# Search and mask rows made inside the top-32 attention, and GpSimd inverting the softmax sums of three attentions

## The reference, cut to what matters

```
x += softmax attention of layernorm(x) on ctx, with biases      l0a
x += mixture of 8 experts, one per token                        l0f
x += ctx aligned to layernorm(x) by dynamic time warping        dtw
x += gated feed-forward layer                                   l1f
x += softmax attention of layernorm(x) on ctx, rotary           l2a
x += mixture of 8 experts, two per token                        l2f
x += attention on ctx that keeps the 32 largest scores per row  l3a
x += attention of layernorm(x) on itself, in two groups         l3f
```

```
q, k, v = x @ W_qkv
sim = mean over the heads of cosine(q[token, head], g[head]), g given
sim = (sim - min) / (max - min)          # over all tokens but 5 registers per batch
pos = sim > 0.9
a token attends to the tokens of its own group and to the 5 registers;
a register's result is the mean of its results on both groups
```

## Time and profile before

| what | us |
|---|---|
| median of 3 runs | 2517.51 |
| lowest and highest run | 2512.94, 2529.06 |
| the profiled execution, its own time | 2528.44 |
| its span, first to last instruction | 2526.6 |

### The profile page before, as it was taken

How to read it: one execution, slowest core, us unless ns; L and a number is a source line. 1 busy time by engine, 2 the same in 40 slices (tenths; PEclk the granted TensorE clock), 3 DMA queues, 4 the chain that set the end, 5 groups by cost and what they waited for, 6 DMA issues and landing times. The chain is left out here.

```text
span 2526.6 us, 40368 instructions
## 1 busy us (share of the span) xinstructions
PE 1999.9 (79%) x13256; PEld 1620.2 (64%) x13256; DVE 1621.2 (64%) x5281; ACT 1161.8 (46%) x3231; POOL 1006.2 (40%) x939
## 2 busy tenths in 40 slices
PE   8996898699948967876999936777777777773887
PEld 5664798599827855555999925555655655562554
DVE  6765111588973246744111179999999999982884
ACT  3552232455321014432333336677777777672443
POOL 3310454300006033303555436666666666652540
PEclk9996999655879989987999956677877877676899
DMA  3111575520304012324364230000000000002232
GB/s 94 64 56 61 211 240 181 142 31 1 143 14 169 0 63 76 101 76 144 127 217 156 85 117 22 9 18 9 24 20 9 18 18 1 18 17 79 74 115 67
DMA packets 102803, 194.94 MB, mean 77 GB/s; under 512 B 20110, under 2 KB 71718, under 8 KB 94630
## 3 DMA queue, kind: packets, MB, share of 16 engines
q1 hardware_dynamic: 78792, 106.90, 13.2%
q0 software_dynamic: 23808, 85.50, 9.8%
HBM read 211.44 MB, written 50.10 MB: 104 GB/s over the span
## 5 line engine op out<-in xcount | busy, mean ns | idle before, releaser
L740 DVE MATCH_REPLACE8 l3a_left<-l3a_top,l3a_left 128x256 f32<-128x256 f32 x768 | 323.3, 448 | 0.0
L733 DVE MAX8 l3a_top<-l3a_left 128x8 f32<-128x256 f32 x768 | 300.1, 451 | 0.0
L466 POOL TENSOR_TENSOR l3a_prob<-l3a_expd,l3a_rest 128x512 f32<-128x512 f32 x128 | 162.9, 1273 | 219.9 <-ACT l3a_rest L548 219.3
L317 PE MATMUL l3a_psT<-all_ident,l3a_prob 128*128 128x128 f32 x512 | 112.5, 360 | 136.6 <-POOL l3a_prob L466 136.0
L335 PEld LDWEIGHTS l3a_psO<-l3a_probT,l3a_vp 128*128 128x128 f32 x1024 | 168.7, 247 | 69.8 <-ACT l3a_probT L564 40.2
L335 PE MATMUL l3a_psO<-l3a_probT,l3a_vp 128*128 128x128 f32 x1024 | 192.2, 346 | 26.0 <-ACT l3a_probT L564 26.0
L453 POOL TENSOR_TENSOR l3a_kept<-l3a_raw_sc,l3a_mone 128x512 f32<-128x512 f32 x128 | 163.4, 1276 | 67.9 <-ACT l3a_raw_sc L532 67.9
L1742 ACT ACTIVATE l2f_hT<-l2f_psH,l2f_wt 128x128 f32<-128x128 f32 x312 | 89.2, 369 | 213.2 <-PE l2f_psH L1673 186.3
L317 PEld LDWEIGHTS l3a_psT<-all_ident,l3a_prob 128*128 128x128 f32 x512 | 77.8, 183 | 155.7 <-POOL l3a_prob L466 155.7
L459 POOL TENSOR_TENSOR l3a_sc_sb<-l3a_kept,l3a_mlow 128x512 f32<-128x512 f32 x128 | 162.9, 1272 | 10.0
L2104 PE MATMUL dtw_psS<-dtw_r,all_shift 128*128 128x1 f32 x596 | 152.9, 357 | 9.8 <-DVE dtw_r L2284 9.4
(11 more groups left out here) (544 smaller groups left out, 4885.1 us busy)
## 6 DMA issues: line engine op xcount, KB each, us to landing
o_at<-l0a_oraw SPq DMA_DIRECT2D x16, 256.0 KB, 2.0
l0a_osum<-o_at SPq DMA_DIRECT2D x32, 128.0 KB
kv_at<-dtw_vd SPq DMA_DIRECT2D x8, 512.0 KB, 2.8
k_at<-dtw_kx SPq DMA_DIRECT2D x8, 512.0 KB, 4.0
l1f_kx<-k_at SPq DMA_DIRECT2D x8, 512.0 KB, 4.5
kv_at<-l1f_k SPq DMA_DIRECT2D x8, 512.0 KB, 3.1
l2a_k<-kv_at SPq DMA_DIRECT2D x8, 512.0 KB, 5.7
l2a_vd<-kv_at SPq DMA_DIRECT2D x8, 512.0 KB, 6.6
```

The costliest lines, as they stand in the source:

```text
L317: mm = nc.tensor.transpose(psT[u % 2][:, kc, e, :], prob[:, u % 4, e, kc * P:kc * P + P], ident[:])
L466: nc.gpsimd.tensor_tensor(prob[:, u % 4, :, :], expd[:, u % 2, :, :], rest[:, u % 2, :, :], ALU.subtract).then_inc(picked, 1)
L733: ins = nc.vector.max(top[:, e, eight], rows[:, e, :] if r else scores[:, e, :])
L740: ins = nc.vector.match_replace(out=rows[:, e, :], in_to_replace=top[:, e, eight], in_values=rows[:, e, :] if r else scores[:, e, :], imm_ ...
```

## The change

- `find_groups` is gone. Its steps are in `picked_attention`: the norm of the vector that the search compares with (`g_sb`) at step 6 of the first batch, the cosines of seven batches behind the loop (`cosines(0, ...)`), those of the last one later, and the search, the two small matmuls and the transposition of the flags between the projections of the last batch. TensorE gets six filler matmuls there (`keep_busy`).
- The queries and keys of l3f are stored already parted into even and odd heads (keys also whole, for the registers). The flags and masks are written into them in DRAM by 16 small DMAs at the end of l3a. So `mrow`, `q_parted` and `k_parted` of l3f, and `load_qk`, are gone; `load_made` loads the parted forms, per batch 512 KB of queries, 512 KB of parted keys, 256 KB of keys and 512 KB of values.
- In l3f, `register_queries` moves from VectorE to GpSimd, `register_read` and `register_half` from VectorE to ScalarE.
- In all three softmax attentions `invert` leaves VectorE. GpSimd computes the inverse ahead of its product, as the power -1 of the sums.
- In the layer norm ahead, the product of mean and reciprocal deviation moves from VectorE to ScalarE.

```diff
@@ picked_attention, SyncE
-                sp.dma_start(ahead["k"][g], a_k[:, g % 2, :, :].rearrange("p c n -> p (c n)")).then_inc(a_out[g % 2], 16)
+                sp.dma_start(ahead["k"][g], a_k[:, g % 2, :, :, :].rearrange("p e c n -> p (e c n)")).then_inc(a_out[g % 2], 16)
...
+            sp.wait_ge(r_done, 1)
+            sp.dma_start(ahead["flags"].rearrange("f (t p) -> (f t) p", p=P), rows[:]).then_inc(flagged, 16)
             for p in range(2):
                 sp.wait_ge(a_out[p], 48 * (B // 2))
+            sp.wait_ge(flagged, 16)
+            for what, f in (("q", 0), ("q", 1), ("k", 2), ("k", 3)):
+                for e in range(2):
+                    at = DK * (1 - e) + 1 + f % 2
+                    free = ahead[what].rearrange("b p (e c n) -> b p e c n", c=DC, n=S)[:, at:P:32, e, :, :]
+                    for c in range(DC):
+                        sp.dma_start(free[:, :, c, :], ahead["flags"][f:f + 1, :].rearrange("o (b n) -> o b n", b=B).to_broadcast([B, P // 32, S]))\
+                            .then_inc(flagged, 16)
+            sp.wait_ge(flagged, 16 * 17)
@@ TensorE, behind the loop
             out_project(NY - 1)
+            pe.wait_ge(a_v_ev, B - 1)
+            keep_busy(nc, made[:].rearrange("p c n -> p (c n)"), ident, 5)
             ahead_turned(B - 1)
+            pe.wait_ge(raw_set, U)
+            keep_busy(nc, psF, ident, 1)
             ahead_made(B - 1, "wq", a_xT_ev, a_q_ps)
             ahead_sims(B - 1)
             ahead_made(B - 1, "wk", a_q_ev, a_k_ps)
+            pe.wait_ge(pT_done, U)
+            pe.wait_ge(e_in, 1)
+            nc.tensor.transpose(psE[0:2, 0:P], ends[:], ident[:]).then_inc(e_turned, 1)
+            pe.wait_ge(e_set, 1)
+            nc.tensor.matmul(psA[:, 0:2], ones[0:2, :], end_by[:], start=True, stop=True).then_inc(e_out, 1)
             ahead_values(B - 1)
+            pe.wait_ge(c_done, 1)
+            nc.tensor.transpose(psF[0:4 * NT, 0:P], col[:].rearrange("p f t -> p (f t)"), ident[:]).then_inc(f_done, 1)
@@ ScalarE, per batch (ahead_normalise, ahead_read_q, ahead_read_k)
+                for t in range(QT):
+                    last = nc.scalar.activation(a_offset[:, g % 2, t:t + 1], a_nm[:, g % 2, t:t + 1], ACT.Copy, scale=a_rstd[:, g % 2, t:t + 1])
...
-                nc.scalar.activation(a_q[:, g % 2, :, :], made[:], ACT.Copy, scale=scale)
+                for e in range(2):
+                    nc.scalar.activation(a_q[:, g % 2, e, :, :], made[:], ACT.Copy, scale=qscale[:, e:e + 1])
...
-                nc.scalar.activation(a_k[:, g % 2, :, :], made[:], ACT.Copy).then_inc(a_k_ev, 1)
+                for e in range(2):
+                    nc.scalar.activation(a_k[:, g % 2, e, :, :], made[:], ACT.Identity, bias=even[:, 2 + e:3 + e], scale=even[:, e:e + 1])
+                nc.scalar.activation(a_k[:, g % 2, 2, :, :], made[:], ACT.Copy).then_inc(a_k_ev, 1)
@@ ScalarE, behind the loop
             read_sums(NY - 1)
+            early_roots()
             read_out(NY - 1)
             ahead_moments(B - 1, 1)
             ahead_normalise(B - 1)
             ahead_read_x(B - 1)
             ahead_read_q(B - 1)
             ahead_read_sims(B - 1)
+            last_roots()
@@ VectorE, behind the loop
             normalise_out(NY - 1)
-            ahead_offsets(B - 1)
+            cosines(0, 0, EARLY)
+            ahead_over(B - 1)
+            cosines(1, EARLY, NT)
+            nc.vector.scalar_tensor_tensor(out=t2[:], in0=reg[:], scalar=BIG, in1=sim[:], op0=ALU.mult, op1=ALU.add)
...
@@ paired_attention, SyncE
+            def load_made(b):
+                if b >= 2:
+                    sp.wait_ge(q2_set, b - 1)
+                    sp.wait_ge(rg_set, b - 1)
+                    sp.wait_ge(s1_done, 16 * (b - 1))
+                sp.dma_start(qd[:, b % 2, :, :, :].rearrange("p e c n -> p (e c n)"), made_at[0][b]).then_inc(q_land[b % 2], 16)
+                if b >= 3:
+                    sp.wait_ge(s2_done, 16 * (b - 2))
+                sp.dma_start(k2[:, b % 3, :, :, :].rearrange("p e c n -> p (e c n)"), made_at[1][b, :, 0:4 * S]).then_inc(k_land[b % 3], 16)
+                if b >= 2:
                     sp.wait_ge(rg_sc, b - 1)
+                sp.dma_start(kf[:, b % 2, :, :].rearrange("p c n -> p (c n)"), made_at[1][b, :, 4 * S:]).then_inc(kf_land[b % 2], 16)
                 if b >= 3:
                     sp.wait_ge(pv_ps, 2 * (b - 2))
                     sp.wait_ge(rg_pv, b - 2)
                 sp.dma_start(vd[:, b % 3, :, :, :].rearrange("p t h m -> p (t h m)"), made_at[2][b]).then_inc(v_land[b % 3], 16)
...
-            if groups is not None:
-                for e in range(2):
-                    for f in range(4):
-                        sp.dma_start(mrow[DK * (1 - e) + 1 + f % 2:P:32, f // 2, e, :], groups[f:f + 1, :].to_broadcast([4, TOK]))\
-                            .then_inc(m_in, 16)
...
-                load_qk(1)
-                for b in range(3):
-                    load_v(b)
+                load_made(1)
             sp.dma_start(W["wo"][:], w["wo"].rearrange("(c p) n -> p c n", p=P)).then_inc(w_in, 16)
...
-                if made_at is not None and y % 2 == 0 and y // 2 + 3 < B:
-                    load_qk(y // 2 + 3)
-                if made_at is not None and y % 2 == 0 and 3 <= y // 2 + 2 < B:
-                    load_v(y // 2 + 2)
+                if made_at is not None and y % 2 == 1 and (y + 5) // 2 < B:
+                    load_made((y + 5) // 2)
                 realign(y)
@@ GpSimd
             def normalise_out(y):
                 b, c = y // 2, y % 2
+                pool.wait_ge(o_in[y % 2], 32 * (y // 2 + 1))
+                nc.gpsimd.tensor_tensor(rinv[:, y % 2, :], osum[:, y % 2, 1, :], minus[:, 0:1].to_broadcast([P, S]), ALU.pow).then_inc(inv_set, 1)
                 pool.wait_ge(inv_set, y + 1)
...
+            def register_queries(b):
+                pool.wait_ge(q_land[b % 2], 16 * (b // 2 + 1))
+                if b:
+                    pool.wait_ge(rg_sc, b)
+                for c in range(DC):
+                    for e in range(2):
+                        ins = nc.gpsimd.tensor_tensor(rg_q[:, c, e:H:2, :], qd[:, b % 2, e, c, 0:REG].unsqueeze(1).to_broadcast([P, H // 2, REG]),
+                                                      rg_sel[:, c, e:H:2].unsqueeze(2).to_broadcast([P, H // 2, REG]), ALU.mult)
@@ VectorE
-            def invert(y):
-                dve.wait_ge(o_in[y % 2], 32 * (y // 2 + 1))
-                if y >= 2:
-                    dve.wait_ge(o_set, y - 1)
-                nc.vector.reciprocal(rinv[:, y % 2, :], osum[:, y % 2, 1, :]).then_inc(inv_set, 1)
```

More of the change, by code:

```diff
@@ L387, in ahead_sims @@
                     rows = slice(t * P, t * P + P)
-                    product(sims_ps[:, t, 0, :], [a_q[:, g % 2, c, rows] for c in range(DC)], [a_gsel[:, c, :] for c in range(DC)])
+                    for e in range(2):
+                        for c in range(DC):
+                            nc.tensor.matmul(sims_ps[:, t, 0, :], a_q[:, g % 2, e, c, rows], a_gsel[:, c, :],
+                                             start=(e == 0 and c == 0), stop=(e == 1 and c == DC - 1))
                     mm = product(sims_ps[:, t, 1, :], [a_sq[:, c, rows] for c in range(DC)], [a_sel[:, c, :] for c in range(DC)])
@@ new lines, in _ @@
+            nc.vector.tensor_scalar(ends[:, 1:2], ends[:, 1:2], -1.0, None, ALU.mult).then_inc(e_in, 1)
+            dve.wait_ge(e_turned, 1)
+            then(nc.vector.tensor_reduce(end[:], psE[0:2, 0:P], AX.X, ALU.max))
+            nc.vector.tensor_scalar(end_by[:], ident[0:2, 0:2], end[:, 0:1], None, ALU.mult).then_inc(e_set, 1)
+            dve.wait_ge(e_out, 1)
+            then(nc.vector.tensor_copy(ends_all[:], psA[:, 0:2]))
+            then(nc.vector.tensor_tensor(span[:], ends_all[:, 0:1], ends_all[:, 1:2], ALU.add))
@@ L1277, in _ @@
             nc.gpsimd.memset(nm[:].rearrange("p b q c n -> p (b q c n)"), 0.0).then_inc(nm_zero, 1)
+            nc.gpsimd.memset(minus[:], -1.0).then_inc(minus_set, 1)
+            pool.wait_ge(minus_set, 1)
             pool.wait_ge(q_in, 16 * n_q)
-            q_parted(0)
-            if kv_at is None:
+            if made_at is None:
+                q_parted(0)
+            if kv_at is None and made_at is None:
                 k_parted(0)
             pool.wait_ge(w_in, 16 * n_w)
+            if made_at is not None:
+                register_queries(0)
             add_bias(0)
@@ L1529, in _ @@
                 b, t = divmod(n, 4)
-                if groups is not None and t == 0 and b < B:
-                    register_queries(b)
                 if n < NQ:
@@ L1551, in _ @@
                     register_probs(b)
-                if groups is not None and t == 3 and b < B:
-                    register_read(b)
                 if groups is not None and t == 1 and 0 <= (n - 13) // 4 < B:
@@ L2702, in program @@
         flags = nc.dram_tensor("flags", (4, TOK), F32, kind="Internal").ap()
[L2703 to L2715 removed]
```

(9 more changed lines are left out.)

287 lines of the change are left out of this document (109 added, 178 removed).

## The result

The changed kernel takes 4152.6 us (median of 4 runs, 4150.85 to 4154.59) against 2523.3 us (4 runs, 2512.94 to 2532.3) for the one before: a ratio of 1.644, with a 95% interval of 1.640 to 1.648. The forecast was 2502 us, with a range of 2480 to 2800. The profiled execution has a span of 4149.2 us.

What follows compares the result with a forecast made beforehand. No engine was taken as always busy: VectorE bounds l3a, a chain of waits the way to l3f, and TensorE l0a. The terms -9 + 1 - 1 - 10 + 4 = -15 us, against the median 2517.5, gave 2502 us, range 2480 to 2800.

Steps and rivals of the forecast that it cites:

- part 3: Inversion on GpSimd in the softmax attentions: a power of 3.0 us (0.73 to 14), hidden except at three ends, +4 us.
- The power is long, and GpSimd becomes the bound: Softmax attentions: GpSimd sets the periods once a power (p) exceeds about 7.5 us; +49 us at 8, +350 at 14; chance 0.40.
- The forecast's own case: Whole kernel: a power of 3.0 us is hidden in the middle of attentions, -15 us in sum; chance 0.41.
- Part 1: From l3a's last output to l3f's first scores: shorter chain of waits, -9 us, bounds -14 and +2.
- -3.3: Between l3a and l3f: fillers keep TensorE's clock up, so queries' and keys' matmuls save 1.65 us each.
- -1.5 for `register_queries`: Start of l3f: this work leaves VectorE's first step, where it took 2.57 us; partly covered, -1.5 us.
- Part 2: Softmax attentions: VectorE without reciprocals, -10 us in l3f (0 to -21), -1 for l0a and l2a together.
- half of 2.7 us a batch: Middle of l3f: at most 2.7 us per period to gain; half taken, 1.4 us over 7 batches, -10 us.
- The loop of l3a, +1: Loop of l3a: VectorE, its bound, gets two instructions on 256 elements and a small one, about +1 us.

Runs made afterwards that it cites:

- the row of kernels: The changed kernel with the power on the first 16, 48 or 128 columns and a product on the rest: 2516.9, 2582.5 and 3186.9 us.
- the rows alone: The changed kernel with the inversion back on VectorE's reciprocal at its old place: 2518.2 us against 2526.9, ratio 0.9968.
- one_product: The changed kernel with a plain product by -1 on GpSimd in place of each power, sums not inverted: 2508.8 us, ratio 0.9924.
- power_16: The changed kernel with the power on 16 of 256 columns and a product by -1 on the other 240: 2516.9 us, ratio 0.9972.
- power_alone: The kernel before the change with only the inversion moved, from VectorE's reciprocal to GpSimd's power: 4186.9 us, ratio 1.657.
- two_queues: Against the rows alone, the eight copies into the stored keys are issued by ScalarE's queue instead of SP's: 2513.1 us, ratio 0.9955.

## Why the prediction was wrong

**The step that failed is the price of the power** in part 3: "I take 3.0 us, as the reciprocal is the nearest thing to a row for it, and keep 0.73 and 14." It is 41.12 us, 13.7 times what I took and 2.9 times the upper bound. The estimate of 3.0 carried VectorE's ratio of reciprocal to product over to another engine. The bound of 14 counted 40 elementary steps with no row behind the 40. No row of the trace had a price for it, and I closed the range all the same at +280 us, a power of 12.6 us. What I left above it, a chance of 0.17, is where the result lies, and nothing in the prediction put a price on a power beyond 14 us.

**The rival was right in its mechanism.** "The power is long, and GpSimd becomes the bound" named the place and the point from which it decides (about 7.5 us; 6.5 to 8.0 by the row of kernels), and its periods at p = 41.1 are 88.8, 88.7 and 86.5 us, against 89.0, 90.2 and 85.9 measured. Its sum there would be 7 x (67.6 + 68.4 + 65.9) + 3 x 110.7 - 10 = +1735 us against +1629 measured. It is too high by 40, 35 and 43 us in l0a, l2a and l3f (543.8, 554.2 and 529.3 us more than before measured), about one power each: seven periods of two powers and three more at the end make 17, and an attention has 16.

**The forecast's own case** can be seen with 16 columns (p = 3.5): -7 us by its ratio (0.28% of 2525) where I had -15 for p = 3.0. That the middle hides such a power is right. The other terms:
- Part 1, -9 forecast, of which -7.8 up to the first scores; there it is -3.4 in the changed kernel and -3.6 in the rows alone. To the values' store: -0.4 forecast, +1.2 measured (21.38 us, where it was 20.19 before). The three sets of eight matmuls cost 9.25 us before (3.64, 3.62, 1.99) and 8.70 with the rows alone (1.98, 2.94, 3.78); the clock that the fillers won for the first set fell again before the keys were done, and the values had the lower level, so -3.3 was -0.5. From that store to the start of l3f: -3.7 forecast, -0.35 measured (17.53 to 17.18 us), with 16 copies at 0.66 us each, not the 0.52 of `mrow`, and 3.6 us of landing and scope behind them, not 2.2. From that start to the scores: 15 us forecast, 14.1 measured (18.6 before), -4.5, the one that I had too small. The -1.5 for `register_queries` came to about -0.3: from the first scores to the first maxima it is 2.2 us with the rows alone and was 2.5.
- Part 2, -10 in l3f and -1 elsewhere: -11 in all by `one_product`, but with a p of 0.6, whose shorter link is part of it, and at the ends, not in the periods. With a p of 3.5, `power_16` stands level with the rows alone. That the sizes of part 2 agree is luck. That reading of "half of 2.7 us a batch" was wrong in place.
- The loop of l3a, +1: from its first pass to its last it is 763.8 us before and with the rows alone. A term of 1 us can't be seen there, as the same loop took 760.0 us in `power_alone`, which has the code of before, and 756.8 us in `power_16`, which has that of the changed kernel.

## What to carry to other kernels

Before an operation is moved to an engine that has never run it in the trace, run that one instruction alone on it; 60% of idle time is room for a 3 us instruction and none for a 41 us one. The room is (period - other work) / count, here 7 us per inversion, and what goes beyond it is paid once per instruction. Then ask what stands behind it in that engine's order: 3.4 us on a half idle ScalarE cost some 67 us (2585.7 less 2518.2), 42 of them in l3f, where links of TensorE's chain waited behind it.

## What the runs showed of the hardware

- GpSimd's power takes 0.35 us + 159 ns per column, whether 16 or 128 partitions are used, whatever the exponent; its product of 128x256 takes 0.61 us.
- VectorE's reduce of the maxima isn't slowed by powers beside it: it has a median of 683 ns in l3f of the changed kernel, where it was 682 before.
- The clock of a set of eight matmuls changed with what TensorE did before it: behind 4.45 us of fillers the queries took 1.98 us in every kernel that has them, without them 3.75. Where the clock falls again isn't fixed by the fillers: the values took 3.78 us in the changed kernel and in the rows alone, but 1.99 in `two_queues` and `one_product`, which have the same fillers and where the keys took the 3.76 us.
